# Routing, choice and merge of a mixture-of-experts layer as one pass over groups of four batches

## The reference, cut to what matters

```
x = x + experts(layernorm(x))
experts:
  logits = x @ gate_w.T + gate_b            # [16, 256 tokens, 32 experts]
  probs  = softmax(logits, over the tokens)
  vals, idx = top 8 tokens of each expert, per batch
  merged[b, e] = sum_k vals[k] * x[b, idx[k]]       # one 512 vector per batch and expert
  h = gelu([merged, 1] @ w1[e]);  o = [h, 1] @ w2[e]  # w1: 32 x 513 x 2048, w2: 32 x 2049 x 512, float32
  out[b, idx[k]] += vals[k] * o
```

## Time and profile before

| | us |
|---|---|
| median of 3 runs | 4003.99 (4002.36 to 4004.89) |
| profiled execution | 4007.67 |
| its span, first to last instruction | 4005.9 |
| busy in the span | PE 3444.4, DVE 1974.0, POOL 1408.4, ACT 1263.5 |
| route, top, merge by their first instructions | 1934.13, 2019.23, 2050.72 |
| experts, first instruction | 2116.04 |
| next phase (norm), first instruction | 2752.70 |

### The profile page before, as it was taken

One profiled execution on the slowest core, in us unless ns is written; L12 is line 12 of the kernel. 1 busy time (PEld: TensorE's weight loads), 2 busy tenths in 40 slices (PEclk: granted clock), 3 DMA queues, 4 the chain that ended last, 5 costly groups with the idle time before them and its releaser, 6 DMA issues. The chain is left out here.

```text
span 4005.9 us, 71048 instructions
## 1 busy us (share of the span) xinstructions
PE 3444.4 (86%) x23116; PEld 2412.7 (60%) x23116; DVE 1974.0 (49%) x4934; ACT 1263.5 (32%) x4320; POOL 1408.4 (35%) x2092
## 2 busy tenths in 40 slices
PE   4999999999997999999667666655999699999955
PEld 3776776776764888888352111113777578888831
DVE  5555554554553665666420000002666466666667
ACT  2222232232222555555100000001111266666621
POOL 2554554554551443343100000000222155555537
PEclk9999999999997999999857877877999799999976
DMA  5000000000002111110459999994121211111113
GB/s 126 22 16 16 31 16 24 24 16 31 16 11 86 36 60 54 50 63 32 164 173 425 427 427 427 427 427 184 69 70 63 83 37 58 42 63 42 53 66 131
DMA packets 158786, 459.15 MB, mean 115 GB/s; under 512 B 47392, under 2 KB 51872, under 8 KB 138208
## 3 DMA queue, kind: packets, MB, share of 16 engines
q1 hardware_dynamic: 150272, 445.72, 29.3%
q10 hardware_dynamic: 8448, 12.59, 0.9%
HBM read 402.17 MB, written 56.10 MB: 114 GB/s over the span
## 5 line engine op out<-in xcount | busy, mean ns | idle before, releaser
L431 POOL TENSOR_TENSOR cross_prob<-cross_prob,cross_rsum 128x256 f32<-128x256 f32 (+1 forms) x1024 | 547.1, 562 | 725.8 <-DVE cross_rsum L816 721.6
L678 ACT ACTIVATE cross_prob<-cross_S,cross_neg_max 128x256 f32<-128x256 f32 (+1 forms) x1024 | 444.1, 457 | 53.6 <-DVE cross_neg_max L811 46.2
L431 POOL TENSOR_TENSOR self_prob<-self_prob,self_rsum 128x128 f32<-128x128 f32 (+1 forms) x512 | 246.3, 506 | 193.7 <-DVE self_rsum L816 189.4
L590 PE MATMUL cross_T<-cross_ident,cross_prob 128*128 128x128 f32 x1792 | 289.1, 278 | 11.0 <-DVE cross_probT L821 7.7
L1217 PE MATMUL experts_H<-moe_w,experts_tok 128*32 128x512 f32 x1024 | 168.7, 818 | 140.2 <-DMA moe_b<-in_L_ffn_w 135.6
L590 PEld LDWEIGHTS cross_T<-cross_ident,cross_prob 128*128 128x128 f32 x1792 | 205.0, 141 | 70.8 <-issue 38.2
L821 DVE COPY cross_probT<-cross_T 128x384 f32<-128x384 f32 (+1 forms) x256 | 158.6, 620 | 165.5 <-PE cross_T L590 165.5
L678 ACT ACTIVATE self_prob<-self_S,self_neg_max 128x128 f32<-128x128 f32 (+1 forms) x512 | 208.9, 422 | 82.6 <-DVE self_neg_max L809 82.6
L534 PE MATMUL self_A<-self_wo_f,self_zT 128*128 128x512 f32 x512 | 225.1, 593 | 0.6 <-DVE self_zT L828 0.6
L1357 POOL MEMSET norm_minus_half<- 128x2 f32 x1 | 0.1, 104 | 636.3 <-POOLq L53 636.3
L678 ACT ACTIVATION_READ_ACCUMULATOR cross_prob<-cross_S,cross_neg_max 128x1 f32 x1024 | 222.5, 217 | 0.0
(11 more groups left out here) (270 smaller groups left out, 8941.6 us busy)
## 6 DMA issues: line engine op xcount, KB each, us to landing
moe_w<-in_L_ffn_w SPq DMA_DIRECT2D x64, 4096.0 KB, 34.8
cross_x_t<-x SPq DMA_DIRECT2D x32, 512.0 KB, 5.1
cross_c_t<-in_ctx SPq DMA_DIRECT2D x32, 512.0 KB, 6.2
cross_res<-x SPq DMA_DIRECT2D x32, 512.0 KB, 3.6
x<-cross_res SPq DMA_DIRECT2D x32, 512.0 KB, 2.8
self_x_t<-in_x SPq DMA_DIRECT2D x16, 512.0 KB, 4.6
self_res<-in_x SPq DMA_DIRECT2D x16, 512.0 KB, 3.5
x<-self_res SPq DMA_DIRECT2D x16, 512.0 KB, 2.8
```

Of the source, the lines that this page charges most:

```text
L431: ins = pool.tensor_tensor(pr, pr, rsum[:, h, t:t + 1].to_broadcast([P, KQ[t]]), ALU.mult)
L590: mm = pe.transpose(TP[:, o:o + P], prob[:, h % NP, SOFF[t] + k * P:SOFF[t] + (k + 1) * P], ident[:, :])
L678: ins = act.activation(prob[:, h % NP, SOFF[t]:SOFF[t] + KQ[t]], SC[h % 4][:, SOFF[t]:SOFF[t] + KQ[t]], ACT.Exp, bias=neg_max[:, h, t:t + ...
```

## The change

The three phases route, top and merge become one, "route", for 16 batches in groups of G = 4.

- Batch n of x is loaded straight into the second weight slots, w1_s[1] for batches 0 to 7 and w2_s[1] for 8 to 15 (`x_of`), normalized there and used from there by the merge. `x_norm`, `logits_d` and `selT_d` are gone.
- SP issues x of batch 0, gate, ident, four copies of the bias, x of the other 15, then w1 and w2 of expert 0, all without a wait; then `sel_d` group by group; w1 of expert 1 after the third group's choice and the second merge; w2 of expert 1 after the last merge.
- DVE takes the statistics of batch n+1 ahead of normalizing batch n. Only the second half of the normalization signals.
- The transposed x of four batches is kept, and the logits of a group are 16 matmuls in four column tiles, so that they come out with 4 batches x 32 experts on the partitions; bias-add and choice act on that in place.
- The merge uses the chosen probabilities as weights (32 columns, one column tile per batch) and x as the moving side with 512 columns: 8 matmuls per group. ACT copies the sums, PE transposes them (4 blocks), DVE copies one 128 x 512 block per group to `merged`.
- All loops of the phase are written out, without `Fori`.

Core of the diff (the new programs of SP, DVE, ACT and PE; the removed phases are in the code above):

```diff
+            XB = [r.bank(f"X{i}") for i in range(2)]
+            TB, M, MT = (r.bank(n) for n in "TMU")
+            def x_of(n):
+                flat = w1_s[1][:, :, :].rearrange("p k j -> p (k j)") if n < HALF else w2_s[1][:, :, :, :].rearrange("p n q m -> p (n q m)")
+                return flat[:, n % HALF * T * D:(n % HALF + 1) * T * D].rearrange("p (t d) -> p t d", t=T)
 sync:
+                sp.dma_start(x_of(0), x_in[0].rearrange("(t p) d -> p t d", p=P)).then_inc(x_ok[0], 16)
+                sp.dma_start(gate[:, :], gate_w).then_inc(const_in, 16)
+                sp.dma_start(ident[:, :], consts["ident"]).then_inc(const_in, 16)
+                for b in range(G):
+                    sp.dma_start(gb[b * E:(b + 1) * E, :], gate_b.rearrange("(e o) -> e o", o=1)).then_inc(const_in, 16)
+                for n in range(1, n_batch):
+                    sp.dma_start(x_of(n), x_in[n].rearrange("(t p) d -> p t d", p=P)).then_inc(x_ok[n], 16)
+                load_w1(sp, 0, 0)
+                load_w2(sp, 0, 0)
+                for g in range(NG):
+                    sp.wait_ge(step, N_STEP * (g + 1))
+                    sp.dma_start(sel_d[g * G:(g + 1) * G].rearrange("b e s -> (b e) s"), pr[:, g, :]).then_inc(stored, 16)
+                    if g == NG // 2:
+                        sp.wait_ge(m_full, NG // 2)
+                        load_w1(sp, 1, 1)
+                sp.wait_ge(m_full, NG)
+                load_w2(sp, 1, 1)
+                sp.wait_ge(stored, 16 * NG)
 vector:
+                def logits_out(g):
+                    dve.wait_ge(l_full, g + 1)
+                    dve.tensor_scalar(pr[:, g, :], L[g % 2][:, 0:S], gb[:, 0:1], None, ALU.add).then_inc(l_ok, 1)
+                    dve.wait_ge(l_ok, g + 1)
+                    dve.tensor_reduce(nm[:, g:g + 1], pr[:, g, :], AX.X, ALU.max, negate=True).then_inc(mx, 1)
+                def merged_out(g):
+                    dve.wait_ge(mt_full, g + 1)
+                    dve.tensor_copy(merged[:, :, :, g * G:(g + 1) * G].rearrange("p e k b -> p k b e"),
+                                    MT[:, :].rearrange("p (k b e) -> p k b e", k=KD, b=G)).then_inc(mt_ok, 1)
+                for n in range(n_batch):
+                    if n + 1 < n_batch:
+                        stats_of(n + 1)
+                    apply(n)
+                    g = n // G - 1
+                    if g >= 0 and n % G == 0:
+                        logits_out(g)
+                    if g >= 0 and n % G == 1:
+                        choose(g)
+                    if g >= 1 and n % G == 0:
+                        merged_out(g - 1)
+                logits_out(NG - 1)
+                merged_out(NG - 2)
+                choose(NG - 1)
+                merged_out(NG - 1)
 scalar:
+                for n in range(n_batch):
+                    g = n // G - 1
+                    if g >= 0 and n % G == 1:
+                        exps(g)
+                    taken(n)
+                    if g >= 0 and n % G == 2:
+                        chosen(g)
+                    if g >= 0 and n % G == 3:
+                        summed(g)
 tensor:
+                def logits(g):
+                    pe.wait_ge(t_ok, 2 * G * (g + 1))
+                    if g >= 2:
+                        pe.wait_ge(l_ok, g - 1)
+                    for k in range(KD):
+                        for b in range(G):
+                            mm = pe.matmul(L[g % 2][b * E:(b + 1) * E, 0:S], gateT[:, k, :], xT[:, b, k, :], start=(k == 0), stop=(k == KD - 1),
+                                           tile_position=(0, b * E))
+                    mm.then_inc(l_full, 1)
+                def merge(g):
+                    pe.wait_ge(sel_ok, g + 1)
+                    if g >= 1:
+                        pe.wait_ge(m_ok, g)
+                    for t in range(T):
+                        for b in range(G):
+                            mm = pe.matmul(M[b * E:(b + 1) * E, :], selT[:, g % 2, t, b * E:(b + 1) * E], x_of(g * G + b)[:, t, :],
+                                           start=(t == 0), stop=(t == T - 1), tile_position=(0, b * E))
+                    mm.then_inc(m_full, 1)
+                for n in range(n_batch):
+                    g = n // G - 1
+                    transposes(n)
+                    if g >= 0 and n % G == 2:
+                        choice(g)
+                    if g >= 0 and n % G == 3:
+                        merge(g)
+                    if n % G == 3:
+                        logits(n // G)
+                        if g >= 0:
+                            to_channels(g)
+                choice(NG - 1)
+                merge(NG - 1)
+                to_channels(NG - 1)
```

More of the change, by code:

```diff
@@ L894, in over_ring, with expert_phase @@
         body(n - r + s, n // r - 1, s, s == r - 1)
[L897 removed]
+def expert_phase(nc, n_batch, x_in, consts, gate_w, gate_b, w1, w2, sel_d, out_d):
     E = gate_w.shape[0]
@@ L943, in expert_phase @@
[L943 to L954 removed]
+            pr = r.sb("pr", [P, NG, S])
@@ L958, in _ @@
                 sp.dma_start(ident[:, :], consts["ident"]).then_inc(const_in, 16)
-                sp.dma_start(gate[:, :], gate_w).then_inc(const_in, 16)
-                sp.dma_start(gb[:, :], gate_b.rearrange("(e o) -> e o", o=1)).then_inc(const_in, 16)
-                def load(n, s):
-                    sp.dma_start(x_t[:, s, :, :], x_in[n].rearrange("(t p) d -> p t d", p=P)).then_inc(x_ok[s], 16)
-                for s in range(2, R):
-                    sp.sem_inc(stored[s], 16)
-                for s in range(2):
-                    load(s, s)
@@ L970, in body @@
-                def body(n, i, s, last):
-                    if not isinstance(n, int) or n + 2 < n_batch:
-                        u = (s + 2) % R
-                        sp.wait_ge(stored[u], 16 + 16 * i)
-                        sp.wait_ge(t_full, 1 + 2 * n)
-                        load(n + 2, u)
-                    sp.wait_ge(l_ok, 1 + n + 1)
-                    sp.dma_start(logits_d[n], lg[:, s % 2, :]).then_inc(l_stored[s % 2], 16)
-                over_ring(sp, n_batch, R, body)
-                for s in range(R):
-                    sp.wait_ge(stored[s], (16 if s >= 2 else 0) + 16 * n_batch // R)
@@ L982, in _ @@
-                for s in range(2):
-                    sp.wait_ge(l_stored[s], 16 + 16 * n_batch // 2)
+                for b in range(G):
[10 more added lines that the diff above has]
+                        load_w1(sp, 1, 1)
@@ new lines, in apply @@
+                def apply(n):
+                    dve.wait_ge(ln_pow, n + 1)
+                    x = x_of(n)
+                    for t in range(T):
+                        ins = dve.tensor_scalar(x[:, t, :], x[:, t, :], mv[:, n % 2, t, 0:1], rstd[:, n % 2, t:t + 1], ALU.subtract, ALU.mult)
+                    ins.then_inc(normed, 1)
+                def logits_out(g):
[3 more added lines that the diff above has]
+                    dve.tensor_reduce(nm[:, g:g + 1], pr[:, g, :], AX.X, ALU.max, negate=True).then_inc(mx, 1)
@@ new lines, in _, with taken, exps, chosen @@
+                logits_out(NG - 1)
+                merged_out(NG - 2)
+                choose(NG - 1)
+                merged_out(NG - 1)
+            @block.scalar
+            def _(act):
+                def taken(n):
+                    if n >= G:
+                        act.wait_ge(l_full, n // G)
+                    for j in range(2):
+                        act.wait_ge(t_full, 2 * n + j + 1)
+                        act.activation(xT[:, n % G, 2 * j:2 * j + 2, :].rearrange("p k n -> p (k n)"), XB[j][:, :], ACT.Copy).then_inc(t_ok, 1)
+                def exps(g):
+                    act.wait_ge(mx, g + 1)
+                    act.activation(pr[:, g, :], pr[:, g, :], ACT.Exp, bias=nm[:, g:g + 1], accum_out=sm[:, g:g + 1]).then_inc(ex, 1)
+                def chosen(g):
+                    act.wait_ge(sel_full, g + 1)
+                    if g >= 2:
+                        act.wait_ge(m_full, g - 1)
+                    act.activation(selT[:, g % 2, :, :].rearrange("p t e -> p (t e)"), TB[:, 0:T * P], ACT.Copy).then_inc(sel_ok, 1)
+                def summed(g):
+                    act.wait_ge(m_full, g + 1)
+                    if g >= 2:
+                        act.wait_ge(mt_full, g - 1)
+                    act.activation(tokens_sb[:, g % 2, :], M[:, :], ACT.Copy).then_inc(m_ok, 1)
+                for n in range(n_batch):
[7 more added lines that the diff above has]
+                        summed(g)
+                exps(NG - 1)
+                chosen(NG - 1)
+                summed(NG - 1)
@@ new lines, in to_channels @@
+                def to_channels(g):
+                    pe.wait_ge(m_ok, g + 1)
+                    if g >= 1:
+                        pe.wait_ge(mt_ok, g)
+                    for k in range(KD):
+                        mm = pe.transpose(MT[:, k * P:(k + 1) * P], tokens_sb[:, g % 2, k::KD], ident[:, :])
```

(4 more changed lines are left out.)

228 lines of the change are left out of this document (58 added, 170 removed).

## The result

The changed kernel takes 3898.26 us (median of 4 runs, 3894.89 to 3901.43) against 4003.63 (4 runs, 4002.36 to 4004.89): 105 us less, ratio 0.9734, 95% interval 0.9722 to 0.9746. Forecast were 3909 and a gain of 95. Its profiled execution took 3899.97 us (span 3898.2), 107.7 less than the 4007.67 before.

What follows compares the result with a forecast made beforehand. Bound by a gapless weight stream: its start and the tensors left count. 76.6 us from the earlier start plus 20.3 from two tensors fewer, less 1.6, gave -95 us: 3909 by the median, range 3890 to 3930.

Steps and rivals of the forecast that it cites:

- M: Time after the last merge when w2 of expert 1 is issued; forecast 2024.6, which gives 76.6 us of the gain.
- The stream: Expert weights from M: 61 tensors at 10.15 us, plus start-up and gap, ending at M + 622.6 us.
- gap of 1 us: DMA pause behind M before w1 of expert 2 flows, that load being issued at M + 11.3; 0 to 4 us.
- The start: Start of the pass: first issue at 1934.13, batch 0 normalized (apply(0)) by 1944.1.
- DVE: DVE's work in the pass: 2.7 us per batch, plus bias-add, maximum, choice 1.91 and copy to merged 1.0 per group.
- The tiles: Four column tiles run together on PE: a group's logits or merge cost 1.9 us at high clock, 3.6 at low.
- rival of tiles in series: Column tiles don't overlap at 256 columns in logits and merge: some 17 us more per group, 3977 us; chance 0.05.
- The clock: PE in the pass: transposes and merge at 1.2 GHz, logits behind the merge at 2.4; DVE waits 3.8, then 4.8 us.
- rival of a clock always high: PE stays at 2.4 GHz throughout the pass: M 12 us earlier, 3897 us; chance 0.13.
- The tail: From the last batch's normalization to M: logits, bias, Exp, choice, transposes, copy and merge at low clock, 15.9 us.
- likeliest case: The forecast's own case for the whole kernel, 3909 us, spanning 3898 to 3917; chance 0.50.
- slower rival: Instruction fetch of the pass's straight-line code waits behind x and weight transfers: 112 us of stalls, 4021 us; chance 0.02.

Runs made afterwards that it cites:

- e1: Changed kernel with expert 0's w1 and w2 issued only after the last merge, leaving 63 tensors instead of 61: 3917.24 us, ratio 0.9783.
- e7: Changed kernel with DVE normalizing each batch right behind its own statistics, as the kernel before did: 3916.93 us, ratio 0.9770.
- e6: Changed kernel with the loops of logits and merge turned round, all products of one column tile before the next: 3916.03 us, ratio 0.9770.
- e2: Changed kernel with half of expert 1's w2 issued after the third merge, the other half after the last: 3904.85 us, ratio 0.9750.
- e4: Changed kernel with eight extra unused transposes after the transposes of three batches out of four: 3897.19 us, ratio 0.9726.
- e5: Changed kernel with logits ahead of the merge in each group's fourth batch and DVE's copy to merged one batch later: 3902.23 us, ratio 0.9742.
- e9: e5 with each group's Exp moved on ACT ahead of the copies of sums and transposed x: 3897.83 us, ratio 0.9736.
- e11: e9 plus half of expert 1's w2 early and unused extra matmuls in PE's pauses and around the last choice: 3893.11 us, ratio 0.9725.

## Why the prediction was right, point by point

- **The mechanism.** Right: the stage's end is the landing of a gapless stream, and the time is set by M and by the tensors left at it. e1 moves the tensors alone (18.7 us for two, forecast 20.3). e7 and e6 move M, by 12.2 and 12.0 us, and the stream stays within 1.3 us of its length, so that the last landing moves as much (pass plus stream 716.9 in both, 13.3 above the 703.6 of the changed kernel; the whole 14 us up by the ratios, 0.0036 x 4004).
- **The stream.** 621.21 us against 622.6 from M. The 11.3 us to w1 of expert 2 came out, and the rate was a little better than 10.15: e1's 63 tensors give (639.86 - 2) / 63 = 10.12 us each. The gap of 1 us is hard to see, from 2022.4 to 2028.4 the DMA moved 384 GB/s instead of some 420, about 0.5 us by my estimate; e2 shows where it comes from.
- **The start.** apply(0) ended 9.7 us behind the first issue (forecast 10.0).
- **DVE.** 2.59 us per batch instead of 2.7, so 1.3 us less in the 12 batches between the bursts' marks and 1.6 in all: from the earlier trace rows I had taken the last small instruction of the statistics with its whole 0.17 us, while the normalization begins 0.07 to 0.08 us behind its start. Choice 1.91 and copy to merged 1.02 are as estimated; bias-add and maximum took 0.85 (estimated 1.0).
- **The tiles.** As forecast: 3.64 and 1.91 us for a group's logits, 3.64 and 1.92 for a merge. The rival of tiles in series fell in the trace, and e6 shows by how much the order of issue could have brought it back.
- **The clock: the mis-sized term.** The prediction had transposes and merge at 1.2 GHz and only the logits at 2.4. DVE's waits were to be 3.8, 4.8 and 4.8 with a burst of 7.5 ahead of the tail; they are 3.83, 2.92 and 2.98, with 6.76. The first group is right to 0.03 us. In the others the clock rose in the transposes ahead of the merge, where the transposes of two batches and the choice's two stood close together (PE 4.13 us busy of the 4.32 from 1964.35 to 1968.67). The three merges ahead of logits took 1.92, 1.92 and 2.00 us where 3.6 was counted, and the waits are shorter by 1.9 + 1.8 + 0.7 = 4.4. The step that failed is "transposes and merge at 1.2 GHz". It rested on the rows and on the Trainium skill, "TensorE: Matmul & The Clock Gate", section Part 4: PE-mode transpose, by which transposes don't count; I weighed that too high, as e4 shows. The truth lies between the forecast and the rival of a clock always high (3897), which by its time alone looks better than the forecast (3898.26 measured) and is not: the first group and the last merge ran at 1.2 GHz.
- **Batch 15, a slip.** The sum gave every batch 2.7 us on DVE. Behind batch 14 there are no statistics left, so batch 15 is normalized directly behind it (first row, from DVE's timeline, four instructions) and was ready 1.5 us sooner. PE was then still busy with batch 14 and the choice, and began batch 15 some 1.1 us late (second row, from PE's). So in the last burst only 0.7 of the 1.8 us that the merge at the high clock gave can be seen.

```profile
1997.28 2.13 DVE L1010 TENSOR_SCALAR moe_w<-moe_w,route_mv,route_rstd 128x512 f32<-128x512 f32 x4
...
2000.53 1.91 PE L1112 MATMUL route_X<-moe_ident,moe_w 128*128 128x128 f32 x8
```

- **The tail.** 8.6 us from the last bias-add to M, 8.4 in the prediction, last merge cold (3.64) as forecast.
- **The sum.** Pass 82.4 instead of 90.5, 8.1 us: the clock (4.4 in the waits), DVE's hand-overs (1.6), batch 15 (1.5), and 0.6 from the start (0.3) and the bias-adds with their maxima (0.4 to 0.5), less 0.2 in the tail. The profile's gain (107.7) exceeds the forecast one (95) by 12.7: these 8.1, 1.4 in the stream (622.6 from M forecast, 621.21 measured), 1.7 ahead and 1.3 behind, together 12.5. The last two are chance: the last expert's products ran at the high clock here (3.64 us) and not when the changed kernel was run again (5.34). The measured 3898.26 lies at the lower edge of what the prediction called the likeliest case (3898 to 3917).
- **Code in straight line.** No wait on code anywhere in the pass: DVE runs without an unexplained gap while DMA is 1.03 busy from 1942 to 1972. The slower rival had nothing to it.
- w1 of expert 1 was issued at 1996.10 and landed ahead of M (DMA 0.10 busy from 2008 to 2012): no cost, as forecast.

## What to carry to other kernels

When a stage is a stream of loads at full bandwidth, look for the moment from which it runs without a gap and count the tensors left at it: everything ahead of that moment counts in full, and each tensor moved ahead of it nearly so (9.3 of 10.15 us here), while bytes moved early behind the same wait (e2) only turn into a gap. Moving one step ahead on an in-order engine moves another behind: e5's gain went to Exp on ACT, much of e9's to the clock, half of e11's to a store standing behind an early transfer; read each engine's waits again after every such edit, ahead of stacking the next one on it.

## What the runs showed of the hardware that I had not expected

- TensorE's clock rose from 1.2 to 2.4 GHz with nothing on it but float32 transposes one behind the other (e4: from 1941.6 on, high at about 1947). With eight per 2.59 us it stayed at the low level (changed kernel, 0.50 from 1942.2 to 1952.5).
- Four instructions in a row to one column tile still overlap with the next tile's (e6: 1.94 us for 16 of 512 columns), eight in a row only in part (4.57 us for 32 of 256, against 1.91 interleaved).
- A store of 128 KB lands late behind loads issued ahead of it on the same queue. Alone it landed in 1.7 us (changed kernel, issued at 2009.92), behind half a w2 with the rest of a w1 ahead of that in 7.6 (e11), and behind the x loads and two tensors in 18.5 (changed kernel, issued at 1961.73).
